# A fused attention and mixture-of-experts kernel: loads of the experts' outputs that wait for the real blocks only, dummy blocks moved to the last experts, and two groups' bases added by VectorE

## The reference, cut to what matters

```python
x = x + xattn(layernorm(x), ctx, ...)
xf = layernorm(x)                                  # [4096, 256]
weights, indices = top_k(softmax(xf @ Wg), 4)      # 4 of 32 experts
for e in range(32):
    out = (silu(xg @ W1[e]) * (xg @ W3[e])) @ W2[e] * w   # xg: the rows that chose e
    y = y.at[tok].add(out)
z = (silu(xf @ Ws1) * (xf @ Ws3)) @ Ws2            # the shared expert
out = x + y + z
```

## Time and profile before

| | us |
|---|---|
| median of 3 runs | 792.35 |
| lowest and highest run | 790.11, 792.65 |
| the profiled execution's own time | 790.2 |
| its span | 788.4 |
| TensorE busy | 746.3 (95%) |
| VectorE busy | 524.1 (66%) |
| ScalarE busy | 464.2 (59%) |
| POOL busy | 379.4 (48%) |
| mean granted clock of TensorE, share of full | 0.985 |

### The profile page before, as it was taken

How to read it: one execution, slowest core, us unless ns; L and a number is a source line. 1 busy time by engine, 2 the same in 40 slices (tenths; PEclk the granted TensorE clock), 3 DMA queues, 4 the chain that set the end, 5 groups by cost and what they waited for, 6 DMA issues and landing times.

```text
span 788.4 us, 18657 instructions
## 1 busy us (share of the span) xinstructions
PE 746.3 (95%) x4222; PEld 593.6 (75%) x4223; DVE 524.1 (66%) x1691; ACT 464.2 (59%) x1820; POOL 379.4 (48%) x352
## 2 busy tenths in 40 slices
PE   6988999999999999999997959999999999999995
PEld 4765777777777777767765639999999999997555
DVE  4864547575869686776866635666666666665588
ACT  2665778777767876766722205666666666666110
POOL 1002332227665666666577553666666666666000
PEclk9999999999999999999999978999999999999999
DMA  9712072325454444499649687677777676664897
GB/s 308 249 53 65 31 249 78 115 94 188 152 168 137 169 147 159 164 313 365 203 132 380 235 317 258 215 215 243 237 225 241 214 242 185 191 191 138 345 411 322
DMA packets 104733, 164.44 MB, mean 209 GB/s; under 512 B 10901, under 2 KB 87779, under 8 KB 103139
## 3 DMA queue, kind: packets, MB, share of 16 engines
q1 hardware_dynamic: 90447, 120.01, 46.3%
q0 software_dynamic: 13824, 41.96, 15.0%
q10 hardware_dynamic: 404, 1.82, 0.6%
HBM read 90.01 MB, written 78.97 MB: 214 GB/s over the span
## 4 chain that ended last, share of the span: by engine, by line
PE 73%; POOL 7%; issue 6%; DVE 6%; ACT 3%; DMA 3%; ACTq 0%; DVEq 0%; SPq 0%; POOLq 0%
PE psum L1751 19%; PE psum L1552 13%; PE psum L1640 12%; PE psum L1488 9%; PE psum L1758 9%; POOL expert_lists L705 5%; PE psum L1672 4%; PE psum L1511 3%; DVE big L1451 2%; ACT sm L857 2%; DMA expert_lists<-rows,slot 2%; PE psum L1687 1%; PE psum L1598 1%; PE psum L1526 1%; POOL sm L719 1%
## 5 line engine op out<-in xcount | busy, mean ns | idle before, releaser
L748 POOL DMA_INDIRECT y_d<-sm,yrow x160 | 156.6, 979 | 107.3 <-DVE yrow L1427 78.1
L1751 PE MATMUL psum<-xbT,w_now 128*128 128x128 f32 x1280 | 172.5, 278 | 0.0
L719 POOL TENSOR_TENSOR sm<-sm,sinv 128x1232 f32<-128x1232 f32 x32 | 71.9, 2248 | 185.6 <-DVE sinv L1076 185.5
L857 ACT ACTIVATE sm<-psum,nmax 128x77 f32<-128x77 f32 x512 | 158.0, 370 | 5.4 <-DVE nmax L1069 5.2
L1751 PEld LDWEIGHTS psum<-xbT,w_now 128*128 128x128 f32 x1280 | 157.2, 193 | 3.2 <-DVE xbT L1420 1.8
L705 POOL DMA_INDIRECT expert_lists<-rows,slot x128 | 126.9, 992 | 57.4 <-issue 35.9
L1640 PE MATMUL psum<-big,pT 128*128 (+1 forms) x640 | 143.6, 379 | 0.0
L1552 PE MATMUL psum<-big,xnT 128*128 (+2 forms) x384 | 138.4, 510 | 0.0
L1640 PEld LDWEIGHTS psum<-big,pT 128*128 128x128 f32 x640 | 119.1, 190 | 14.9
L857 ACT ACTIVATION_READ_ACCUMULATOR sm<-psum,nmax 128x1 f32 x512 | 128.8, 252 | 0.0
L1552 PEld LDWEIGHTS psum<-big,xnT 128*128 128x128 f32 x384 | 70.3, 190 | 56.0 <-issue 50.5
(11 more groups left out here) (192 smaller groups left out, 993.7 us busy)
## 6 DMA issues: line engine op xcount, KB each, us to landing
xblk<-expert_lists SPq DMA_DIRECT2D x160, 160.0 KB, 2.3
y_d<-zero SPq DMA_DIRECT2D x32, 512.0 KB, 3.8
big<-y_d SPq DMA_DIRECT2D x8, 2048.0 KB, 16.2
big<-in_L_ffn_W SPq DMA_DIRECT2D x16, 320.0 KB, 6.5
xin<-in_x SPq DMA_DIRECT2D x36, 128.0 KB, 2.4
xres<-in_x SPq DMA_DIRECT2D x8, 512.0 KB, 5.5
x_d<-x SPq DMA_DIRECT2D x8, 512.0 KB, 3.1
xn2T_d<-xn2T SPq DMA_DIRECT2D x8, 512.0 KB, 3.0
```

Of the source, the lines that this page charges most:

```text
L719: pool.tensor_tensor(e3, e3, sinv[:, t % 2, :].unsqueeze(2).to_broadcast([P, NH, SK]), ALU.mult).then_inc(s["probs_ready"], 1)
L748: pool.indirect_dma_start(out=y_d, out_offset=bass.IndirectOffsetOnAxis(ap=yrow[:, q:q + 1], axis=0), in_=eo[:, q, :], in_offset=None).the ...
L857: last = nc.scalar.activation(sm[:, t % 2, h * SK:(h + 1) * SK], head_scores(h, h + 1), ACT.Exp, bias=nmax[:, t % 2, h:h + 1], accum_out=s ...
L1751: last = mm(bank(2 + q % 2)[:, i * P:(i + 1) * P], w_now[:, q % 2, i, k, :], xbT[:, q % 2, k, :], start=k == 0, stop=k == KC - 1)
```

## The change

It has four parts. VectorE computes, after the table, 16 times the number of turns that hold real blocks (`landed_i`), SP loads that into a register, and waits for `scattered[q]` to reach it instead of waiting for all blocks and all scatters; the wait for all scatters is moved behind the last store. Since dummy blocks may then still run while y is loaded over experts' weights, the table's third row gives dummies the experts 31 to 24 (block number modulo 8). TensorE's first `s_up` waits for the last `eh` instead of the last `eo`; the wait for the last `eo` stands before `s_down(5)`. And only groups 6 and 7 (`BY_PE`) have their base added by TensorE; VectorE adds it in the sums of groups 4 and 5, and the order of sums and gates on VectorE changes.

```diff
--- before.py
+++ after.py
@@ -74,6 +74,9 @@
     EARLY = 5
     MID = NG // 2
     RING = 4
+    BY_PE = (NG - 2, NG - 1)
+
+    assert RING * TOPK * TG * D <= (E - NX - 1) * EW
     assert BLOCKS % PE_TURN == 0 and PE_TURN % NX == 0 and BLOCKS % ACT_TURN == 0 and LAG <= PACK and E <= 256
     assert YPAIRS == NT * GT and NG == 2 * B and KC == 2 and HS == 2 * P and H == P and SB == 3 and BLOCKS <= 2 * P and TG * D == E * E and P % E == 0 and E & (E - 1) == 0
 
@@ -171,6 +174,7 @@
         blocks_upto = sb("blocks_upto", [P, E])
         past = sb("past", [P, 2, E])
         pastn = sb("pastn", [P, 2, E])
+        landed_i = sb("landed_i", [P, 3], I32)
         tabw = sb("tabw", [P, 8, 2])
         tabf = sb("tabf", [P, 2, 3])
         tab = sb("tab", [3, BLOCKS], I32)
@@ -266,7 +270,7 @@
             logits_psum logits_sbuf lmax_ready lshifted lexped lsum_ready linv_ready prob_ready top_ready topi_ready
             topf_ready onehot_ready mask2_ready mask_ready gsum2_ready gsum_ready earlier_ready prefix_psum pos_sbuf base_ready
             slot_e_ready picked_ready slotf_ready slot_ready choice2_ready choice_ready rows_of_y_ready pair_ready
-            count_psum tab_step fill_ready tab_psum tab_ready
+            count_psum tab_step fill_ready landed_step tab_psum tab_ready
             s_psum s_silu s_gated z_psum z_added
             xbT_psum xbT_sbuf eh_psum eg_ready eh_ready w1_ready w3_ready yrow_ready eo_psum eo_ready
             ysum_step""".split()}
@@ -448,7 +452,7 @@
                                   ).then_inc(s["filled"], 16)
 
 
-        sums_upto = list(itertools.accumulate(TOPK if g < MID else TOPK - 1 for g in range(NG)))
+        sums_upto = list(itertools.accumulate(TOPK - 1 if g in BY_PE else TOPK for g in range(NG)))
 
         def summed(eng, g):
             if g < MID:
@@ -635,9 +639,12 @@
                 load_turn(i)
 
 
-            sp.wait_ge(s["eo_psum"], BLOCKS)
+
+            sp.wait_ge(s["landed_step"], 3)
+            landed = sp.alloc_register("landed")
+            sp.reg_load(landed, landed_i[0:1, 2:3])
             for q in range(NX):
-                sp.wait_ge(scattered[q], 16 * TURNS)
+                sp.wait_ge(scattered[q], landed)
 
             def load_y(g):
                 if g >= RING:
@@ -656,6 +663,8 @@
                 if g + RING < NG:
                     load_y(g + RING)
                 store_final(g)
+            for q in range(NX):
+                sp.wait_ge(scattered[q], 16 * TURNS)
             for p in range(RING):
                 sp.wait_ge(stored[p], 16 * NG // RING)
 
@@ -1399,7 +1408,7 @@
             tab_op(nc.vector.tensor_scalar(tabf[:, :, 1], expert, float(E - 1), None, ALU.min))
 
             tab_op(nc.vector.tensor_scalar(past_end, expert, float(E), None, ALU.is_ge))
-            tab_op(nc.vector.tensor_scalar(block_e[:, :], block_m[:, :], E - 1, None, ALU.bitwise_and))
+            tab_op(nc.vector.tensor_scalar(block_e[:, :], block_m[:, :], NX - 1, None, ALU.bitwise_and))
             tab_op(nc.vector.tensor_copy(turn_e, block_e[:, :]))
             tab_op(nc.vector.tensor_tensor(turned, past_end, turn_e, ALU.mult))
             tab_op(nc.vector.tensor_tensor(tabf[:, :, 2], tabf[:, :, 1], turned, ALU.subtract))
@@ -1410,6 +1419,14 @@
             nc.vector.tensor_copy(tab[:, :], o_ps[0:3, 0:BLOCKS]).then_inc(s["tab_ready"], 1)
             nc.vector.tensor_copy(tabp[:, :].bitcast(U8)[:, PACK:PACK + BLOCKS], o_ps[0:3, 0:BLOCKS]
                                   ).then_inc(s["tab_ready"], 1)
+
+            nc.vector.tensor_scalar(landed_i[:, 0:1], blocks_upto[:, E - 1:E], float(NX - 1), None, ALU.add
+                                    ).then_inc(s["landed_step"], 1)
+            dve.wait_ge(s["landed_step"], 1)
+            nc.vector.tensor_scalar(landed_i[:, 1:2], landed_i[:, 0:1], NX.bit_length() - 1, None,
+                                    ALU.logical_shift_right).then_inc(s["landed_step"], 1)
+            dve.wait_ge(s["landed_step"], 2)
+            nc.vector.tensor_scalar(landed_i[:, 2:3], landed_i[:, 1:2], 16.0, None, ALU.mult).then_inc(s["landed_step"], 1)
             add_shared(3)
             phase1_over(dve)
             dve.wait_ge(s["tab_ready"], 2)
@@ -1437,7 +1454,7 @@
 
             def sum_group(g):
                 p = g % RING
-                terms = [base[:, g * TG:(g + 1) * TG, :]] if g < MID else []
+                terms = [] if g in BY_PE else [base[:, g * TG:(g + 1) * TG, :]]
                 terms += [ysum[:, p, :, k, :] for k in range(TOPK)]
                 wait(dve, ld_y[p], (g // RING + 1) * 16)
                 so_far, done = terms[0], sums_upto[g] - len(terms) + 1
@@ -1461,21 +1478,22 @@
 
 
             dve.wait_ge(s["ld_base"], 16 * NG)
+            sum_group(0)
             shared_gate(MID, 0)
             shared_gate(MID, 1)
+            sum_group(1)
             shared_gate(MID + 1, 0)
-            sum_group(0)
-            sum_group(1)
+            sum_group(2)
             shared_gate(MID + 1, 1)
             shared_gate(MID + 2, 0)
-            sum_group(2)
             sum_group(3)
+            sum_group(MID)
             shared_gate(MID + 2, 1)
             shared_gate(MID + 3, 0)
-            sum_group(MID)
+            sum_group(MID + 1)
             shared_gate(MID + 3, 1)
             assert NG == 2 * MID == MID + 4
-            for g in range(MID + 1, NG):
+            for g in range(MID + 2, NG):
                 sum_group(g)
 
 
@@ -1685,8 +1703,8 @@
                     z = bank(z_bank(g) + t // 2)[:, t % 2 * D:(t % 2 + 1) * D]
                     for c in range(KC):
                         last = mm(z, hT[:, c, :].rearrange("p (n t) -> p t n", t=TG)[:, t, :], ws2[:, c, :],
-                                  start=c == 0, stop=c == KC - 1 and g < MID)
-                    if g >= MID:
+                                  start=c == 0, stop=c == KC - 1 and g not in BY_PE)
+                    if g in BY_PE:
                         last = mm(z, ident[:, :], base[:, g * TG + t, :], start=False, stop=True)
                     if t % 2:
                         last.then_inc(s["z_psum"], 1)
@@ -1761,7 +1779,7 @@
             turns(pe, {0: block_T, AT_UP: block_up, LAG: block_down}, (0, AT_UP, LAG), PE_TURN,
                   packed_table(pe, "expert", 1, PE_TURN))
 
-            pe.wait_ge(s["eo_ready"], BLOCKS)
+            pe.wait_ge(s["eh_ready"], BLOCKS)
             pe.wait_ge(s["ld_base"], 16 * NG)
             s_up(MID, 0)
             s_up(MID, 1)
@@ -1769,6 +1787,7 @@
             s_down(MID)
             s_up(MID + 1, 1)
             s_up(MID + 2, 0)
+            pe.wait_ge(s["eo_ready"], BLOCKS)
             s_down(MID + 1)
             s_up(MID + 2, 1)
             s_up(MID + 3, 0)
```

## The result

The changed kernel takes 785.45 us (median of 5 runs, 783.18 to 786.74) against 790.38 of the kernel before (5 runs, 789.82 to 792.65): ratio 0.9928, 95% interval 0.9903 to 0.9952 (the ratio is taken over the runs and is not the quotient of the two medians). The profiled execution took 783.18, the least of the five, with a span of 781.4. The forecast was 784.8.

The account below looks back on a forecast made before the run. TensorE's shared products, then VectorE's sums, were taken to bound the tail. 790.2 less a 6.5 us gain gave 783.7; as the shown median lay above the profiled execution, the forecast was 784.8, between 783.7 and 785.9, range 781.5 to 789.5.

Parts of the forecast that it names:

- The sum: Whole kernel: 790.2 us (span 788.4 plus 1.8 around it) less the gain of 6.5 gives 783.7.
- 1. The count: SP's wait before y: 144 real blocks, so no wait; y loads start between 718.6 and 719.7 instead of 732.13.
- 2. When y arrives: Load 0 of y, beside the last scatters, lands between 726.4 and 730.0; 728.2 was taken.
- 3. Dummy experts: Dummy blocks' copies from other columns and scatters hitting the same rows twice: no cost, since no duration changes.
- 4. TensorE: First s_up starts at 727.01, 1.11 us earlier; dropping groups 4 and 5's identity products saves 1.72 each.
- 5. VectorE's order: VectorE's tail: gate(6,0) at 748.96, then work without a gap to 778.75 instead of 785.33; gain 6.58 us.
- the list: Predicted VectorE starts, from gate(6,0) at 748.96 through gates and sums to the end at 778.75.
- 6. Sum 0 in time: Sum 0, now before gate(4,0): load 0 may land up to 728.1; each us beyond costs one; 728.2 costs 0.1.
- The rule against it: VectorE's sum 0 adds could be blocked by POOL's last two scatters, making the gain 4.6 instead of 6.5.
- Slower: Rival, chance 0.07: y loads still start at 732.13, so sum 0 delays the chain; 5.3 us slower, 796.6.
- More: Rival, chance 0.10: VectorE alone sets the tail, or transfers were the bound before; 782 to 784.
- A late first sum: Rival, chance 0.14: sum 0 is held by scatters, a late load or an instruction block; 787 to 789.

Follow-up runs that it names:

- e1: The changed kernel with only the early y loads and dummy experts kept; orders, TensorE's wait and identity products as before: 792.28 us, ratio 1.0012.
- e3: The changed kernel with TensorE's old wait for the last eo before its first s_up: 785.86 us, one run.
- e4: The changed kernel with the base of group 5 added by TensorE again: 782.95 us, ratio 0.9886.
- e5: The changed kernel with SP also waiting for block 159's down product before loading y: 794.92 us, one run.
- e8: The changed kernel without the early y, with TensorE doing 13 unneeded products while it would idle before s_up(5,0): 795.74 us, one run.
- e2: The changed kernel without the early y: SP's old wait for all blocks and scatters, new orders kept; 797.88 us, ratio 1.0089.
- e0: The changed kernel with the count loaded into a register with stated bounds (16 to 320): 783.87 us, ratio 0.9904.
- the cut sums: The changed kernel with VectorE's sums of groups 1, 3 and 5 split to fill its waits before gates: 780.24 us; six more runs 781.24 us.

## Why the prediction was right

The sum gave 783.7 for the profiled execution, which took 783.18. The tail fell by 6.57 of the expected 6.58 us, and the rest is the 0.44 ahead of it. That the median lies only 0.65 above the forecast is in part luck. The median gain is 4.93 us, less than the 6.5 of the sum and than the 7.55 that lie between 784.8 and the median shown then (792.35), which came down by 1.97 with two more runs. The interval (3.8 to 7.7 us) holds all three. The mechanism rests on the starts in the tail, not on the median.

**1. The count** gave no wait, as 144 blocks should: y was issued 1.37 us after the last xblk load, at the lower end of my 1.4 to 2.5, since the register load took 0.54 us, near the lower of my two bounds, and the nine waits, for which I had no row, the 0.50 that is left of 718.15 - 717.11. The three operations took 0.13, 0.15 and 0.15 us, and VectorE's idle time behind them only fell from 3.00 to 2.88.

**2. When y arrives.** Load 0 landed 8.4 us after its issue, and sum 0 began 9.81 us into the tail. My bounds come to 9.2 and 12.8 there (726.4 and 730.0), and I took 10.98, 1.2 too late. I had stretched the load by the scatters' share of the DMA time; it was rather the scatters that lost (below). The load was slowed by 0.6 us, from 7.8 to 8.4. Nothing hung on it, as gate(4,0) had its limit at 10.88. That the only awaited one, block 151's, was in time stands: block 159's yrow is at 723.08, 6.30 into the tail as before (723.52 - 717.22). I named no row for the 4.9 us that I gave each further load; the slowest of loads 0 to 3 took 24.7 us, so all were there by about 744.2, near the 743 that I had.

**3. Dummy experts.** Nothing, as e1 shows together with the early y: ratio 1.0012.

**4. TensorE.** Its first s_up stands at 9.88 instead of 9.79. The 1.1 us are confirmed by e3 (one run), the 1.72 of s_down(4) by 5.44 - 3.72.

**5. VectorE's order.** Every start from gate(6,0) to the end came within 0.02 us of the list. This part and the TensorE part carry the gain, 3.72 and 2.85 us. The added add of group 5 is a cost within it (e4).

**6. Sum 0 in time.** Yes. The limit of 10.88 us is supported by e5, e8 and e2: from it, 61.54 + 8.56 + the clock = 72.6, 61.54 + 12.08 = 73.62 (73.56 measured in e8).

**The rule against it.** POOL's scatter at 726.64 was stretched to 2.02 us beside VectorE's add of 726.59, which kept its 1.23. The Trainium skill ("SBUF — State Buffer", Who interferes with whom) has the second to issue blocked, and the trace agrees: VectorE issued first. The scatters at 728.97 and 730.24 kept 0.97 though, beside adds of the same kind. The other executions show what sets the cases apart (POOL and VectorE in e3):

```profile
727.06 0.97 POOL L756 DMA_INDIRECT y_d<-sm,yrow  x1 [0.48 <-ACT sm L987]
...
727.45 1.23 DVE L1467 TENSOR_TENSOR big<-big,base 128x1024 f32<-128x1024 f32 x1 [1.71 <-DMA big<-y_d]
...
728.33 1.19 POOL L756 DMA_INDIRECT y_d<-sm,yrow  x1 [0.30 <-ACT sm L987]
```

A scatter that starts during an add is longer by what is left of that add, less some 0.13 us: in the changed kernel 1.18 us were left and it grew by 1.05, in e3 0.35 and 0.22, in e0 0.31 and 0.18 (727.40, 1.15 us), in the kernel before 0.93 and 0.81. The two that kept 0.97 started with about 0.1 us left. That covers each case seen; no run was made to test it. The other way round nothing was lost: the add of 727.45 started 0.39 us into a scatter and kept its 1.23 us, and in e4 one that started 0.18 us into a scatter (729.32 and 729.14) did so too. In that order, which the rival needed, the traces do not show the second to issue blocked.

**The rivals.** *Slower* is real: e2 is it, with its mechanism, place and point. Its price was mis-sized, 7.9 us of tail instead of 5.3. The term that was missing is TensorE's clock after idle time, 2.4 us by e2 and e8; the rest is sum 0 at 22.90 where I had 22.73. If the clock falls, the change loses from T0 = 728.1 + 6.58 - 2.4 = 732.3 on and not from 734.7 (an estimate: in the runs sum 0 starts either before 10.5 us of the tail or after 19, never between). *More*, with the transfers as the bound of before, fell with e1. *A late first sum* didn't occur.

What I had wrong without harm: I let s_up(7,1) take 3.5 us after an idle time of 3 us. It took 5.35, and 6.74 in e0. In the prediction's sum the term for the clock was nothing. The forecast held because VectorE was busy meanwhile; e0 shows a tail 1.1 us longer for it. That the profiled execution met the list within 0.02 us is luck in this respect.

## What to carry to other kernels

An earlier transfer is worth what the order behind it makes of it: alone it brought nothing (ratio 1.0012), the order alone lost (1.0089), together they gained (0.9928). Price a tail by following, point by point, which engine arrives last; here that gave each start within 0.02 us. Where an order leaves TensorE idle for a few us, look at its granted clock behind the gap before pricing the next products, and prefer an order, like the cut sums, that leaves no gap.

## What the runs showed that I had not expected

**TensorE's clock.** Behind these idle times the granted clock fell to one half, the lower of its two levels (1.2 of 2.4 GHz), and the s_up behind took longer than its 3.60 us:

| execution | idle, us | s_up behind it, us |
|---|---|---|
| changed kernel | 2.80 | 5.35 |
| e8, before s_up(7,1) | 2.80 | 5.37 |
| e3 | 2.80 | 6.72 |
| e0 | 2.80 | 6.74 |
| e5 | 8.26 | 6.19 |
| e2 | 11.73 | 6.15 |

After 1.08 (e4) and 0.63 us (e8, before s_up(5,0)) it did not fall. In e1, after 2.58 us, it was 0.50 in 771 to 774, but not in the kernel before after 2.57. In e2 and e5 it did not fall after a second gap, of 2.80 us (s_up(7,1) 3.67 in both). So gaps of about this length go either way: of six of 2.80 us, four were followed by the half clock, and the two that were not are those of the executions in which the clock had already fallen once in the tail. Whether that matters was not tried. I had seen the gap of before pass without it and had not thought further.

**Scatters beside loads.** In 717 to 731 of the changed kernel, a scatter landed 9.8 to 10.3 us after its issue, against a median of 2.4 (the profile gives this for some of the scatters only):

```profile
DMA to landing us min/median/max: 9.8/10.0/10.3
```

They share the DMA engines with 8 MB of queued loads of y. The Trainium skill, "DMA: Bandwidth & Descriptors", Queues, rings and completion order, says that each engine takes turns between its queues, packet by packet. No view here shows the turns themselves; what the trace shows is that a small transfer does not stay quick beside the loads: it took four times as long. Nobody waits for these scatters here. Had SP started the loads two or three blocks earlier, yrow and eo of the last blocks might have had to wait for them; that was not tried.
